# Folding once instead of twice, two-column roots, and stages placed for each engine, in a fused transformer kernel with an FFT autocorrelation block

## The reference

```
# layer 1 (attention), then:
hidden = silu(x @ gate_w.T) * (x @ up_w.T);  out = hidden @ down_w.T      # layer 2, 1792 wide
f = rfft(xh); corr = irfft(f * conj(f), n=512)                            # layer 3, each row
weights, delay = top_k(corr, 6);  tmp = softmax(weights)
out = sum_k tmp_k * roll(x, -delay_k)
gate = x @ gate_w.T + (x @ gate_a.T) @ gate_b.T; up, down likewise        # layer 4, 1376 wide
_layernorm(x) = (x - mean) / sqrt(var + 1e-5)
```

## Time and profile before

| | |
|---|---|
| median of 3 runs | 913.89 us (913.09 to 918.67) |
| the profiled execution | 920.06 us, of it the span 918.0 us |
| TensorE matmuls busy | 749.4 us, 82% of the span |
| VectorE busy | 670.1 us, 73% |
| ScalarE, GpSimd busy | 363.9 us, 291.7 us |
| TensorE and VectorE busy from 480 to 918 us | 370.45 and 350.00 of 438 us |
| mean granted clock of TensorE | 0.908 |

### The profile page before, as it was taken

The page is one execution under the profiler, slowest core; times in us unless marked ns, Lnnn a source line. Parts: engine busy times, 40 slices in busy tenths (PEclk is TensorE's granted clock), DMA queues, the critical chain, the costliest instruction groups (busy, mean ns, idle before and its releaser), DMA issues. The chain is left out here.

```text
span 918.0 us, 16061 instructions
## 1 busy us (share of the span) xinstructions
PE 749.4 (82%) x5081; PEld 408.7 (45%) x5102; DVE 670.1 (73%) x1781; ACT 363.9 (40%) x699; POOL 291.7 (32%) x348
## 2 busy tenths in 40 slices
PE   1967666879898898988869998696969999788694
PEld 1623221223222222222327676474747777566472
DVE  7523875766776767797489999896998999955713
ACT  1212224545565545677104444343433534323121
POOL 4024443102021120232104555345524335224131
PEclk9988656989899999998979999898989999899798
DMA  9499889772131312644451375613645221110100
GB/s 265 74 177 341 237 245 225 150 165 60 29 60 28 49 39 39 154 121 135 107 159 25 98 141 109 187 24 86 81 98 94 43 35 25 24 46 1 46 24 24
DMA packets 144477, 93.38 MB, mean 102 GB/s; under 512 B 111832, under 2 KB 123224, under 8 KB 144200
## 3 DMA queue, kind: packets, MB, share of 16 engines
q1 hardware_dynamic: 133360, 70.19, 34.4%
q10 hardware_dynamic: 10816, 16.91, 5.9%
q0 software_dynamic: 240, 5.51, 2.9%
HBM read 48.47 MB, written 29.04 MB: 84 GB/s over the span
## 5 line engine op out<-in xcount | busy, mean ns | idle before, releaser
L1205 PE MATMUL ps<-arena 128*128 128x256 f16 (+1 forms) x1952 | 238.2, 279 | 23.9 <-DMA arena<-arena 23.9
L1205 PEld LDWEIGHTS ps<-arena 128*128 128x128 f16 (+1 forms) x1952 | 196.4, 101 | 68.5 <-DMA arena<-arena 16.9
L1432 ACT ACTIVATE arena<-ps 128x1024 f32<-128x1024 f32 (+7 forms) x256 | 163.6, 651 | 123.4 <-PE ps L1462 118.8
L1453 PE MATMUL ps<-arena 96*128 (+4 forms) x384 | 137.0, 382 | 39.9 <-DVE mx L1369 15.5
L1365 DVE CUSTOM_DVE_ANT_0 arena<-ps,arena 128x256 bf16<-128x256 f32 (+3 forms) x256 | 122.0, 488 | 57.2 <-PE ps L1453 49.4
L1057 POOL TENSOR_TENSOR arena<-arena 128x256 f32<-128x256 f32 (+1 forms) x100 | 80.3, 803 | 258.3 <-ACT arena L948 257.6
L1227 PE MATMUL ps<-arena 128*128 128x512 f16 (+2 forms) x467 | 119.6, 385 | 32.6 <-POOL arena L1063 31.2
L1462 PE MATMUL ps<-arena 99*128 (+4 forms) x384 | 128.6, 352 | 4.6 <-ACT arena L1432 4.2
L1340 POOL TENSOR_SCALAR_AFFINE_SELECT arena<-arena 128x512 f32<-128x512 f32 x64 | 42.2, 659 | 230.4 <-ACT arena L1432 230.2
L1369 DVE TENSOR_REDUCE mx<-ps 128x1 f32<-128x512 f32 x128 | 88.2, 689 | 32.1 <-PE ps L1453 31.2
L1453 PEld LDWEIGHTS ps<-arena 96*128 (+1 forms) x384 | 39.3, 102 | 150.0 <-issue 81.0
(11 more groups left out here) (163 smaller groups left out, 851.9 us busy)
## 6 DMA issues: line engine op xcount, KB each, us to landing
arena<-qp_d SPq DMA_DIRECT2D x48, 128.0 KB, 4.1
lora_d<-arena ACTq DMA_DIRECT2D x20, 256.0 KB, 4.5
arena<-lora_d SPq DMA_DIRECT2D x10, 512.0 KB, 5.1
w1n_d<-arena SPq DMA_DIRECT2D x10, 512.0 KB, 3.6
arena<-rec_d SPq DMA_DIRECT2D x32, 128.0 KB, 2.6
qp_d<-arena SPq DMA_DIRECT2D x12, 256.0 KB, 4.9
w1dn_d<-arena SPq DMA_DIRECT2D x4, 704.0 KB, 3.8
arena<-in_L_ffn_down_w_dram ACTq DMA_DIRECT2D x16, 172.0 KB, 3.6
```

The lines of the kernel that those rows point to most:

```text
L1205: last = nc.tensor.matmul(ps[0:h, b, CH * o:CH * (o + 1)], w(t[0])[:, kt, ht * P:ht * P + h], xt[:, c, t[1], kt, :], start=(kt, t) == (0, ...
L1432: nc.scalar.activation(probs[:, kt % 2, h, kt * P:T], st_bank(h).rearrange("p b n -> p (b n)")[:, kt * P:T], ACT.Exp, scale=HD ** -0.5).th ...
L1453: nc.tensor.matmul(s_bank(g, u)[:, 0:k1 - k0], qt6[0:QROWS, g % RING, h, qt * P:(qt + 1) * P], kt6[0:QROWS, g, k0:k1], start=True, stop=Tr ...
```

## The change

- Folding stops after the first step: the second fold and its counterpart after the inverse transform go (`fold`, `unfold`). The tables for the odd frequencies become 256 long, and `FORWARD` and `BACK` have full-size products.
- The rows of layer 3 are folded as they are and scaled by the root while their pieces are made (`scaled_pieces`); the mean isn't subtracted. The zero-frequency column of the cosine table is 0 instead.
- The root works on both columns at once, by three chained instructions a step (`rsqrt`), and the scale XS is put into the variance. The running shift of the mean is replaced by the mean of the first normalisation (`mean0`) and a difference, which `last_norm` adds.
- Each engine gets a table of its own for its share of a stage, and the numbers change.
- The inverse table is loaded in two parts, later; SyncE's order changes at two places; `prepare_down(0)` and `last_norm(0)` change places on VectorE's list.

```diff
-FORWARD = ((0, 0), (0, 1), (1, 2), (2, 0), (2, 1), (3, 3))
-BACK = (((0, 0), (2, D // 2), 0, D // 2), ((1, D), D // 2, P), ((3, D + P), D // 2 + P, P))
+FORWARD = ((0, 0), (0, 1), (1, 2), (1, 3), (2, 0), (2, 1), (3, 2), (3, 3))
+BACK = (((0, 0), (2, D // 2), 0), ((1, D), (3, D + D // 2), D // 2))
...
-        ROWS_AT = (26, 45, 64, 76)
-        CORR_AT = (28, 49, 65, 77)
...
+        ROWS_AT = (27, 46, 64, 76)
+        CORR_AT = (29, 48, 65, 76)
+        SPEC_AT = (38, 58, 69, 80)
+        BACK_AT = (47, 62, 74, 83)
+        TAKE_AT = (28, 46, 64, 76)
+        LAGS_AT = (29, 54, 66, 77)
+        WTAKE_AT = (39, 58, 69, 80)
+        PROD_AT = (43, 60, 73, 82)
+        BTAKE_AT = (47, 62, 74, 83)
+        PLOW_AT = (28, 46, 64, 76)
+        QLOW_AT = (45, 60, 73, 82)
...
+            sp.dma_start(inv_sb[0], inverse[0]).then_inc(tables_loaded, 16)
             w1_transpose(sp, w1g[:, 0], 0, 0)
             transposes(sp, "ffn", 0)
+            down_store(sp, 0)
+            sp.dma_start(inv_sb[1], inverse[1]).then_inc(inverse_loaded, 16)
             w1_transpose(sp, w1g[:, 1], 1, 0)
             transposes(sp, "attn", 3)
-            down_store(sp, 0)
+            down_store(sp, 1)
             w1_transpose(sp, w1u[:, 0], 2, 1)
-            down_store(sp, 1)
...
-            link(nc.vector.tensor_scalar(var[:, 0:SUB], mv[:, 0:SUB, 1], LN_EPS, -0.5, ALU.add, ALU.mult))
-            rsqrt_by_column(link, SUB)
+            link(nc.vector.tensor_scalar(var[:, 0:SUB], mv[:, 0:SUB, 1], gain ** -2, LN_EPS * gain ** -2, ALU.mult, ALU.add))
+            rsqrt(link, SUB)
...
-            shifted(link, c, shift[:, SUB * c:SUB * (c + 1)], first)
+            link.settle()
             row_stats(link, x[:, SUB * c:SUB * (c + 1), :])
-            moments(link)
-            link(nc.vector.tensor_scalar(rstd[:, 0:SUB], rstd[:, 0:SUB], XS, None, ALU.mult))
...
+            moments(link, XS)
...
-            normalised_rows(link, c)
-            fold(link)
-            pieces(dve, link, use_of("ffn", c))
+            fold(link, x[:, SUB * c:SUB * (c + 1), :])
+            scaled_pieces(dve, link, use_of("ffn", c))
...
-            nc.vector.tensor_tensor(xc, xc, y, ALU.add).then_inc(x_done, 1)
-            dve.wait_ge(x_done, c + 1)
+            for i in range(SUB):
+                nc.vector.scalar_tensor_tensor(out=xc[:, i, :], in0=xc[:, i, :], scalar=late_shift[:, i:i + 1], in1=y[:, i, :],
+                                               op0=ALU.add, op1=ALU.add).then_inc(x_done, 1)
+            dve.wait_ge(x_done, SUB * (c + 1))
...
-            link(nc.vector.tensor_tensor(low, low, high, ALU.add))
-            rising, falling = odd[:, :, 1:P], odd[:, :, H2 - 1:P:-1]
-            link.later(nc.vector.tensor_tensor(y[:, :, H2 + 1:H2 + P], rising, falling, ALU.subtract))
-            link.later(nc.vector.tensor_tensor(y[:, :, H2 + P:D - 1], rising, falling, ALU.add))
-            link(nc.vector.tensor_copy(y[:, :, H2:D:H2 - 1], odd[:, :, 0:H2:P]))
+        def fold(link, of):
+
+            low, top_half = of[:, :, 0:H2], of[:, :, H2:D]
+            link.later(nc.vector.tensor_tensor(y[:, :, 0:H2], low, top_half, ALU.add))
+            link(nc.vector.tensor_tensor(y[:, :, H2:D], low, top_half, ALU.subtract))
...
-            link.later(nc.vector.tensor_tensor(odd[:, :, 1:P], cosine, sine, ALU.add))
-            link.later(nc.vector.tensor_tensor(odd[:, :, H2 - 1:P:-1], sine, cosine, ALU.subtract))
-            link(nc.vector.tensor_copy(odd[:, :, 0:H2:P], z[:, :, H2:D:H2 - 1]))
+            even, odd = wback[:, :, 0:H2], wback[:, :, H2:D]
...
+        def scaled_pieces(dve, link, use):
+
+            if use > 1:
+                dve.wait_ge(tr_done[use - 2], 16 * SUB)
+            for i in range(SUB):
+                link.later(nc.vector.tensor_scalar(nat[:, use % 2, i, 0, :], y[:, i, :], rstd[:, i:i + 1], None, ALU.mult))
+            link.settle()
+            for i in range(SUB):
+                nc.vector.scalar_tensor_tensor(out=nat[:, use % 2, i, 1, :], in0=y[:, i, :], scalar=rstd[:, i:i + 1],
+                                               in1=nat[:, use % 2, i, 0, :], op0=ALU.mult, op1=ALU.subtract).then_inc(nat_ready, 1)
...
             after_ffn(dve, link, 0)
+            prepare_down(dve, link, 0)
             dve.wait_ge(late_row_loaded, 16)
             after_attention(dve, link, 3)
-            prepare_down(dve, link, 0)
             peaks(dve, link, 0)
...
             peaks(dve, link, 3)
+            lag_weights(dve, link, 3)
             last_norm(dve, link, 0)
-            lag_weights(dve, link, 3)
             spectra(dve, link, 3)
...
-    low, rising, falling = n[:half], n[:P], n[1:P + 1]
+    low = n[:half]
     cosines, sines = np.cos(angle(low, even)), np.sin(angle(low, even))
     sines[:, 0] = np.cos(angle(low, [half]))[:, 0]
-    forward = np.concatenate([cosines, np.cos(angle(rising, odd)), sines, np.sin(angle(falling, odd))], 0)
+    cosines[:, 0] = 0.0
+    forward = np.concatenate([cosines, np.cos(angle(low, odd)), sines, np.sin(angle(low, odd))], 0)
```

98 lines of the change are left out of this document (36 added, 62 removed).

## The result

The changed kernel takes 887.59 us in the median of 6 runs (885.71 to 894.87), the kernel before 917.77 in 6 runs beside it (913.09 to 919.02): ratio 0.9686 with a 95% interval from 0.9649 to 0.9723, and 30 us less by the medians. (The ratio is estimated from the single runs and is not the quotient of the two medians, which is 0.9671.) A second measurement of both on another chip gave 0.9646 (0.9597 to 0.9695; 888.33 against 918.60), again 30 us by the medians. The forecast was 39 us less (875). The sign, the range and the main mechanism held; a quarter of the gain did not come, and one of the causes named for the waits that stay was wrong. Since the median of before moved from 913.89 to 917.77 with more runs, 4 us of the distance between 875 and 887.59 belong to the anchor and 9 to the reasoning.

The account below looks back on a forecast made before the run. VectorE's list sets TensorE's six late arrivals, TensorE's list the rest. Terms: -42.4 - 12 - 6 + 17 + 7.8 - 2 - 1 = -38.6, taken as -39 from a 913.89 us median: 875 us, range 856 to 893.

Parts of the forecast that it names:

- VectorE's sum: VectorE's list up to the end of `lag_weights(3)`: 48 us shorter, ending at 761 instead of 809.5 us.
- The six waits: Six idle places of TensorE in the feed-forward stretch: 42.4 us go, with 12 us of slow matmuls behind them.
- (a): Tiles 27 to 31, chunk 0: spectrum work some 3 us late for the correlation, then `lag_terms(0)` costs some 4 us.
- (b): Tile 54: a 1.5 us wait stays, VectorE and TensorE within 1 us of each other.
- (c): Tile 58: a 1 us wait, since lag-weight pieces queue behind the first two `w1d` transposes.
- (d): Tile 76: both products of chunk 3 stand there with no tile between to cover the powers, 3.3 us.
- (e): The two later `lag_terms` stages: 2 us of waiting stay.
- B: Rival: the remaining stalls are mostly covered, TensorE running two tiles ahead of ScalarE; 12 of 17 us go, 863 us; chance 0.16.
- A: Rival: contention eats the VectorE gain, each root at its upper end of 3.2 us; 889 us; chance 0.17.
- C: Rival: one large stall stays under another name, such as late last transposes, 8 us, together with A: 897 us; chance 0.08.
- D: Rival: slower than now because of the two-column root, 929 us at 0.6 us an instruction; chance 0.03.
- E: Rival: SyncE's transpose queue is the bound, so only the 9.3 us of `last_norm(0)` are won: 905 us; chance 0.04.

Follow-up runs that it names:

- again: The changed kernel, unaltered, measured a second time on another chip against the kernel before: ratio 0.9646, 888.33 us against 918.60.
- the peaks first and the earlier take: Changed kernel with ScalarE's and GpSimd's share of chunk 0's spectrum at tile 27 and `prepare_down(0)` behind the first peaks: ratio 0.9667 to the kernel before.

## Why the prediction was right in sign and too high in size

**Who bounds.** Right. VectorE's list and TensorE's list shared the path before; after the change VectorE waits for TensorE and ScalarE, and 18 us less on VectorE change nothing that the runs can tell.

**VectorE's sum.** About right in total. Of the 48 us, 36 were work that disappears (the rest were the 9.3 of `last_norm(0)` and 2.6 of a load); its busy time in the stretch fell by 34.3 and 32.7. The root, the term with the widest bounds, came out at 0.2 to 0.35 us for 0.4 from start to end (0.45 in busy time).

**The rule on shared ports.** Two neighbouring instructions of a new root, and GpSimd's instructions at the same time:

```profile
559.97 0.67 DVE L231 SCALAR_TENSOR_TENSOR nw<-nw,var 128x2 f32<-128x2 f32 x1
560.68 0.59 DVE L233 SCALAR_TENSOR_TENSOR rstd<-nw,rstd 128x2 f32<-128x2 f32 x1
```

```profile
559.90 0.72 POOL L1039 TENSOR_TENSOR arena<-arena 128x256 f32<-128x256 f32 x1 [1.57 <-ACT arena L930]
560.58 0.67 POOL L1045 TENSOR_TENSOR arena<-arena 128x256 f16<-128x256 f32 x1
```

The first VectorE instruction takes 0.67 us where its like takes 0.16, and ends at 560.64, GpSimd's at 560.62; the second ends at 561.27, GpSimd's at 561.25. The Trainium skill says in "SBUF — State Buffer", section "Who interferes with whom", that the one that comes second is blocked for the whole of the other; the trace agrees to 0.02 us. By that rule the prediction let the root lose instead of gain. It gains a little all the same, because only few of its instructions are held up: the other seven of this root take 0.16 us each, and the mean over 72 of a kind is 191 to 258 ns.

**The six waits.** Right: at the six places 42.4 us stood, with 12 us of slow matmuls behind them (the rows there give 12.4). Four are gone but for 0.57 us; two are shorter, 3.93 and 3.49 us, and stand in the next term, as the prediction had it.

**The waits that stay, and the clock behind them.** This is the step that failed. It said "With 2 us of slow clock after (a) that is 17 us": 15 us of waits and 2 of slow matmuls. The waits at the places it names are 2.42, 3.93, 3.49, 3.44, twice 0.88, 1.07 and 0.57, together 16.7 us, and 16.8 in the second execution: nearly right. The slow matmuls behind them are 8.9 and 6.4 us instead of 2, since they stand behind all four larger waits and I gave them to one place. So the term is 25.6 and 23.2 us, where 17 stood: 9 and 6 us more, about what is missing in all from the first tile to the last down product (9.5 and 6.0):

| | forecast | changed | again |
|---|---|---|---|
| TensorE's waits | -33.4 | -29.5 | -30.2 |
| transforms (12 times 0.65) | +7.8 | +7.8 | +7.8 |
| slow matmuls | -10 | -4.4 | -7.2 |
| sum | -35.6 | -26.1 | -29.6 |

(The forecast's waits are minus 42.4, minus 6, plus 15; its slow matmuls minus 12, plus 2.) Two smaller errors nearly cancel: of the small stalls 3.8 and 4.6 us went instead of 6, and slow matmuls elsewhere shrank by 1 to 2 us more than I had counted. The row that could have told me stands in the earlier trace rows: the wait of 3.80 us before cost as much in slow matmuls (3.80 instead of 2.13) as that of 11.13 (4.55 instead of 2.78). A wait that shrinks from 8 to 3.5 us gives back 4.5 us, and little or nothing of the slow matmuls behind it: 1.6 us behind the 8.18 before, 1.7 behind the 3.93 now; 2.2 behind the 7.65, 2.7 and 1.7 behind the 3.49.

**Single places.** (a) 7 us expected, 6.35 and 6.86 measured. The cause was half right: in the first execution ScalarE waits 4.4 us there for peaks that stand behind `prepare_down(0)`, which the change had moved ahead; with the peaks first and the earlier take 3.59 us are left, the way round itself. (b) 1.5 us expected at tile 54, 3.49 measured, with 1.7 to 2.7 of slow matmuls. The cause was wrong: it is not VectorE but ScalarE's 4.8 us with two table loads, as the kernel without them showed. (c) 1 us expected at tile 58, none there, but 1.07 and 0.64 us at the weights' transform of chunk 2. (d) 3.3 expected, 3.44 measured, with 1.4 to 2.9 us of slow matmuls that were not counted. (e) 2 us expected, 0.88 twice.

**The signs that it named.** Met: the waits before L630 (5.5 and 7.4 us at chunks 1 and 2 for the 7 and 9 expected), no wait above 5 us, the root's means, and 2.78 us for the transforms that stand behind no wait. The largest waits are near tiles 30 and 76, as said, and at 54 just as large. Not met: the first tile of chunk 3 in layer 4 starts without a wait, but at 835.71 and 830.38 us, not near 818. Counted from the first tile it comes 24 and 28 us earlier than before, where the walk had 41 for the whole way. And one sign of being wrong occurred: TensorE does wait for pieces before the weights' transforms of chunks 2 and 3, though for no more than 1.07 us. The prediction itself had put down 1 us of this, so the sign was drawn too narrowly.

**The ends.** The last chain was right: no wait with six tiles of cover, 8.52 us with three. The tail fell by 1.1 us (918.0 less 903.81 before, 893.1 less 880.00 after), 1 expected. The 2 us of an earlier start are not to be seen, since the first tile's start varies by 12 us. B, that the stalls are mostly covered, is out; A, C, D and E did not happen either.
